# Value tiles of a Perceiver block's cross-attention: the tails of two batches in one tile

## What is computed

```
x = x + xattn(layernorm(x), ctx)          # 16 heads of 32; the change lies here
x = x + linear_attention(layernorm(x))
x = x + top2_of_8_experts(layernorm(x))

xattn:  q = xn @ Wq + bq;  kv = ctx @ Wkv + bkv      # k and v interleaved in the last axis
        p = softmax(q k^T / sqrt(32));  o = p v;  out = o @ Wout + bout
```

## Time and profile before

| | us |
|---|---|
| median of 3 runs | 2366.27 |
| lowest and highest | 2365.36, 2366.97 |
| the profiled execution | 2365.71 |
| its span | 2364.0 |
| TensorE matmuls busy (12921) | 2278.3 (96%) |
| weight loads | 1985.5 (84%) |
| VectorE busy | 1345.2 (57%) |
| GpSimd busy | 1109.5 (47%) |
| ScalarE busy | 1036.3 (44%) |

### The profile page before, as it was taken

How to read it: one execution, slowest core, us unless ns; L and a number is a source line. 1 busy time by engine, 2 the same in 40 slices (tenths; PEclk the granted TensorE clock), 3 DMA queues, 4 the chain that set the end, 5 groups by cost and what they waited for, 6 DMA issues and landing times. The chain is left out here.

```text
span 2364.0 us, 37285 instructions
## 1 busy us (share of the span) xinstructions
PE 2278.3 (96%) x12921; PEld 1985.5 (84%) x12921; DVE 1345.2 (57%) x2111; ACT 1036.3 (44%) x1737; POOL 1109.5 (47%) x456
## 2 busy tenths in 40 slices
PE   8999999999999999999999999999998897899996
PEld 7688889898888888898888888898876686888885
DVE  3155655565655656565656556565667546766652
ACT  3154444444444444444444444444445321545443
POOL 2155555454555555555554555554556202533334
PEclk9999999999999999999999999999999998999998
DMA  4212111121111121111111111121140102856643
GB/s 145 96 53 56 47 48 45 49 63 50 48 47 48 47 59 58 48 45 49 58 55 47 47 48 45 53 66 48 45 132 19 39 25 107 244 179 194 189 149 83
DMA packets 141464, 175.61 MB, mean 74 GB/s; under 512 B 81600, under 2 KB 105024, under 8 KB 141248
## 3 DMA queue, kind: packets, MB, share of 16 engines
q1 hardware_dynamic: 132352, 147.37, 20.7%
q10 hardware_dynamic: 4608, 16.78, 2.2%
q0 software_dynamic: 4288, 8.67, 1.8%
HBM read 135.12 MB, written 37.65 MB: 73 GB/s over the span
## 5 line engine op out<-in xcount | busy, mean ns | idle before, releaser
L504 POOL TENSOR_TENSOR k_parts<-k_t,k_parts 64x1602 fp32r<-64x1602 f32 x128 | 436.8, 3412 | 720.1 <-DVE k_parts L588 720.1
L960 PE MATMUL ps_kv<-ctx_hi,wk_hi 128*128 128x384 f32 (+1 forms) x1024 | 376.0, 367 | 9.3 <-DVE ctx_lo L785 9.3
L652 DVE TENSOR_TENSOR probs_t<-ps_pt,probs_t 128x512 fp32r<-128x512 f32 x376 | 207.7, 553 | 277.3 <-ACT probs_t L830 275.9
L960 PE MATMUL ps_kv<-ctx_hi,wk_lo 128*128 128x384 f32 (+1 forms) x1024 | 352.7, 344 | 0.0
L960 PE MATMUL ps_kv<-ctx_lo,wk_hi 128*128 128x384 f32 (+1 forms) x1024 | 352.7, 344 | 0.0
L960 PE MATMUL ps_kv<-wv_hi,ctx_hi 128*128 128x512 f32 (+1 forms) x832 | 342.8, 412 | 0.6 <-DVE wv_lo L755 0.6
L960 PE MATMUL ps_kv<-wv_lo,ctx_hi 128*128 128x512 f32 (+1 forms) x832 | 330.5, 397 | 0.0
L960 PE MATMUL ps_kv<-wv_hi,ctx_lo 128*128 128x512 f32 (+1 forms) x832 | 326.3, 392 | 0.0
L838 ACT ACTIVATE probs_both<-ps_s,neg_max 128x1601 f32<-128x1601 f32 x128 | 205.1, 1602 | 178.9 <-DVE neg_max L638 178.9
L818 ACT ACTIVATE k_t<-ps_kv,bk_sb 128x384 f32<-128x384 f32 (+1 forms) x256 | 152.5, 596 | 294.8 <-PE ps_kv L960 294.8
L493 POOL TENSOR_TENSOR ctx_lo<-ctx_raw,ctx_hi 128x1536 fp32r<-128x1536 f32 (+1 forms) x64 | 233.7, 3651 | 86.0 <-DVE ctx_hi L577 84.6
(11 more groups left out here) (315 smaller groups left out, 4079.3 us busy)
## 6 DMA issues: line engine op xcount, KB each, us to landing
ctx_raw<-ctx_dram SPq DMA_DIRECT2D x49, 768.0 KB, 4.7
w_raw<-w_dram SPq DMA_DIRECT2D x64, 512.0 KB, 4.5
rows_in<-zeros SPq DMA_DIRECT2D x150, 128.0 KB, 4.1
w_raw<-w_dram ACTq DMA_DIRECT2D x32, 512.0 KB, 4.5
ctx_raw<-ctx_dram SPq DMA_DIRECT2D x16, 900.0 KB, 4.9
q_blocks<-q_parts SPq DMA_DIRECT2D x256, 32.0 KB, 2.4
rows<-rows_in SPq DMA_DIRECT2D x8, 768.0 KB, 4.7
q_parts<-probs_t SPq DMA_DIRECT2D x16, 256.0 KB, 2.0
```

Of the source, the lines that this page charges most:

```text
L504: nc.gpsimd.tensor_tensor(k_parts[64 - 64 * s:128 - 64 * s, :], k_t[par][64 * s:64 * s + 64, g, :], k_parts[64 * s:64 * s + 64, :].bitcast ...
L652: nc.vector.tensor_tensor(probs_t[0:m, j:j + k, 1, :], ps_turned[kv][g][0:m, 0:k, :], probs_t[0:m, j:j + k, 0, :].bitcast(F32), ALU.subtra ...
L960: last = nc.tensor.matmul(o, still, moving, start=(k == 0 and i == 0), stop=(k == DT - 1 and i == 2))
```

## The change

Odd batches no longer make their thirteenth value unit. The last value tile of an even batch b has 128 context columns instead of 65: its own last 65 rows and 63 of the 65 last rows of batch b+1 (unit kind "T"). The result is copied whole into `v[0]`, and two DMA transfers on SP then bring the odd batch's rows to `v[1]`: 63 rows from `v[0]`'s partitions 65 to 127, and 2 rows from a small array in DRAM, `ends_v`. These last two rows of all eight odd batches (16 rows) are made by one small group of 12 matmuls at the beginning, ahead of unit 14 (`values_of_ends`).

The columns of a T unit come from an array `tails` of their own (2304 bytes in each of 128 partitions a batch), laid out on the host, with its own buffers `tail_raw`, `tail_hi`, `tail_lo`, loaded in pair 1 and split in pair 3 of odd batches (`TAILS_AT`), and once at the start. For odd batches unit 27 counts twice in `kv_done` and `kv_copied`, so that all later counts stay as they are.

```diff
+ENDS = 2 * (TAIL - P // 2) * (B // 2)
+TAIL_W = DT * (P + ENDS)
-    vs = [("V", min(j * P // CW, CHUNKS - 1), j) for j in range(JT)]
+    vs = [("V", j * P // CW, j) for j in range(JT - 1)] + [("T", CHUNKS - 1, JT - 1)]
...
+        TURN_FROM, QUERY_FROM, ENDS_FROM = 8, 16, 14
+        ends = o_t[0:ENDS].rearrange("p g c -> p (g c)")
+        ends_bank = ps_s[0:ENDS, 3 * BANK:4 * BANK]
...
+        TAILS_AT = 3
+        def has_unit(par, n):
+            return par == 0 or n < NU - 1
+        def units_ended(par, n):
+            return 2 if par == 1 and n == NU - 2 else 1
...
         @block.sync
+            def load_tails(b):
+                if positive(b):
+                    sp.wait_ge(kv_done, NU * (b - 1))
+                sp.dma_start(tail_raw[:], tails[b] if isinstance(b, int) else tails[bass.ds(b, 1)].rearrange("a p n -> (a p) n")
+                             ).then_inc(tail_loaded, 16)
+            def move_tails(b):
+                sp.wait_ge(kv_copied, NU * b)
+                sp.wait_ge(moved, 16)
+                if positive(b - 1):
+                    sp.wait_ge(v_lo_done, PAIRS * (b - 1))
+                half = TAIL - 2
+                sp.dma_start(v[1][0:half, JT - 1, :], v[0][TAIL:P, JT - 1, :]).then_inc(moved, 16)
+                sp.dma_start(v[1][half:TAIL, JT - 1, :], ends_v[bass.ds(b - 1, 2), :]).then_inc(moved, 16)
...
+                    if p == 2 and par == 0:
+                        move_tails(b + 1)
+                    if p == 1 and par == 1:
+                        load_tails(b + 1)
...
             sp.dma_start(wq_sb, wq.rearrange("(t p) n -> p t n", p=P)).then_inc(wq_loaded, 16)
+            load_tails(0)
             for c in range(2, CHUNKS):
                 load_ctx(0, c)
+            sp.wait_ge(w_hi_done, DT + 2)
+            sp.dma_start(ends_v, ends).then_inc(moved, 16)
...
         @block.gpsimd
+            def split_tails(b):
+                pool.wait_ge(tail_hi_done, b + 2)
+                nc.gpsimd.tensor_tensor(tail_lo[:], tail_raw[:], tail_hi[:].bitcast(F32), ALU.subtract
+                                        ).then_inc(tail_lo_done, 2)
+                pool.wait_ge(tail_lo_done, b + 2)
...
+                    if p == TAILS_AT and par == 1:
+                        pool.wait_ge(k_lo_done, n + 3)
+                        pool.wait_ge(ctx_lo_done, chunks)
+                        split_tails(b + 1)
...
-            for c in range(1, CHUNKS):
+            split_ctx(0, 1, 0)
+            pool.wait_ge(ctx_lo_done, 2)
+            split_tails(0)
+            for c in range(2, CHUNKS):
...
         @block.vector
+            def round_tails(b):
+                dve.wait_ge(tail_loaded, 8 * (b + 2))
+                nc.vector.tensor_copy(tail_hi[:], tail_raw[:]).then_inc(tail_hi_done, 2)
...
                     for b_of, c in splits_at(b, p, kv):
                         split_ctx(b_of, c)
+                    if p == TAILS_AT and par == 1:
+                        round_tails(b + 1)
...
             split_ctx(0, 1)
+            round_tails(0)
             norm_x()
...
         @block.scalar
+                elif kind == "T":
+                    if positive(b):
+                        act.wait_ge(moved, 16 + 16 * b)
+                    nc.scalar.copy(v[par][:, which, :], ps_kv[bank][:]).then_inc(kv_copied, 1)
...
                 if p == 0:
                     act.wait_ge(kv_copied, NU * (b + 1))
+                    if par == 1:
+                        act.wait_ge(moved, 16 + 16 * (b + 1))
...
+                    if k == ENDS_FROM:
+                        nc.scalar.copy(ends, ends_bank).then_inc(w_hi_done, 1)
...
         @block.tensor
+                if kind == "T":
+                    pe.wait_ge(tail_lo_done, b + 2)
...
+                    elif kind == "T":
+                        o, tile = bank[:], slice(k * P, (k + 1) * P)
+                        passes = [(tail_hi[:, tile], wv_hi[:, k, :]), (tail_hi[:, tile], wv_lo[:, k, :]),
+                                  (tail_lo[:, tile], wv_hi[:, k, :])]
...
-                last.then_inc(kv_done, 1)
+                last.then_inc(kv_done, units_ended(par, n))
+            def values_of_ends():
+                pe.wait_ge(tail_lo_done, 2)
+                for k in range(DT):
+                    hi, lo = (part[:, DT * P + k * ENDS:DT * P + (k + 1) * ENDS] for part in (tail_hi, tail_lo))
+                    for i, (still, moving) in enumerate([(hi, wv_hi), (hi, wv_lo), (lo, wv_hi)]):
+                        nc.tensor.matmul(ends_bank, still, moving[:, k, :], start=(k == 0 and i == 0),
+                                         stop=(k == DT - 1 and i == 2))
...
                         for u in AT[p][gap] if kv else ():
-                            unit(b + 1, 1 - par, u)
+                            if has_unit(1 - par, u):
+                                unit(b + 1, 1 - par, u)
...
+                    if k == 3:
+                        pe.wait_ge(w_hi_done, DT + 2)
```

More of the change, by code:

```diff
@@ L116 @@
 LAST = CHUNKS - 1
-START += [unit for g in range(DT) for unit in (("K", LAST, g), ("V", LAST, JT - DT + g))]
+START += [unit for g in range(DT) for unit in (("K", LAST, g), ("V" if g < DT - 1 else "T", LAST, JT - DT + g))]
 START_LAST_OF_CHUNK = [max(n for n, u in enumerate(START) if u[1] == c) for c in range(CHUNKS)]
@@ L131, in positive, with build @@
     return not isinstance(value, int) or value > 0
-def build(nc, x, ctx, wq, bq, wk, wv, bk, bv, wout, bout, lwq, lwk, lwv, lwo, router, w1, w2, out):
+def build(nc, x, ctx, tails, wq, bq, wk, wv, bk, bv, wout, bout, lwq, lwk, lwv, lwo, router, w1, w2, out):
     q_parts = nc.dram_tensor("q_parts", (2, D, NT), F32, kind="Internal").ap()
@@ L137, in build @@
     inv_t = nc.dram_tensor("inv_t", (B, PAIRS, 2, LQ), F32, kind="Internal").ap()
+    ends_v = nc.dram_tensor("ends_v", (ENDS, D), F32, kind="Internal").ap()
     rows_in = nc.dram_tensor("rows_in", ((B - 1) * ZERO_PIECES * ZERO_ROWS, D), F32, kind="Internal").ap()
@@ L142, in build @@
         shared = Shared(nc)
-        cross_attention(nc, ident, shared, x, ctx, wq, bq, wk, wv, bk, bv, wout, bout, lwq, lwk,
-                        q_parts, attn_t, inv_t, rows_in)
+        cross_attention(nc, ident, shared, x, ctx, tails, wq, bq, wk, wv, bk, bv, wout, bout, lwq, lwk,
+                        q_parts, attn_t, inv_t, ends_v, rows_in)
         m = Tail(nc, whole, shared)
@@ L209, in cross_attention @@
             ctx_raw.append(nc.alloc_sbuf_tensor_at(f"ctx_raw{i}", shape, F32, offset=at))
+        tail_hi = sb("tail_hi", [P, TAIL_W], F32R)
+        at = -(-nc.sbuf_base // 32) * 32
+        tail_lo = mem.enter_context(nc.sbuf_tensor("tail_lo", [P, TAIL_W], F32R, align_bytes=32))
+        tail_raw = nc.alloc_sbuf_tensor_at("tail_raw", [P, TAIL_W], F32, offset=at)
         k_t, v = [sb("k_t0", [P, DT, LC2])], [sb("v0", [P, JT, D])]
@@ L287, in cross_attention @@
         rows_zeroed = sem("rows_zeroed")
+        tail_loaded, tail_hi_done, tail_lo_done, moved = sem("tail_loaded"), sem("tail_hi"), sem("tail_lo"), sem("moved")
         wout_loaded, bout_loaded, lwq_loaded, lwk_loaded = (
@@ L316, in start_steps @@
                     yield "scores", 0
+                if u == ENDS_FROM:
+                    yield "ends", 0
                 yield "unit", u
@@ L661, in batch @@
                         dve.wait_ge(o_stored, 64 * b)
+                    elif p == 1:
+                        dve.wait_ge(moved, 16)
                     if positive(n):
@@ L819, in copy_unit @@
                                          bias=bk_sb[:, which:which + 1]).then_inc(kv_copied, 1)
+                elif kind == "T":
+                    if positive(b):
+                        act.wait_ge(moved, 16 + 16 * b)
+                    nc.scalar.copy(v[par][:, which, :], ps_kv[bank][:]).then_inc(kv_copied, 1)
                 else:
                     m = rows(which)
-                    nc.scalar.copy(v[par][0:m, which, :], ps_kv[bank][0:m, :]).then_inc(kv_copied, 1)
+                    nc.scalar.copy(v[par][0:m, which, :], ps_kv[bank][0:m, :]).then_inc(kv_copied, units_ended(par, n))
             def copy_group(n, g, kv):
@@ L915, in _ @@
                         nc.scalar.activation(std[:], std[:], ACT.Sqrt).then_inc(std_done, 1)
+                    if k == ENDS_FROM:
+                        nc.scalar.copy(ends, ends_bank).then_inc(w_hi_done, 1)
                 elif kind == "exponent":
                     exponent(0, 0)
-                elif kind == "scores":
+                elif kind in ("scores", "ends"):
                     pass
@@ L939, in unit @@
                 bank = ps_kv[(NU * par + n) % 2]
-                if n == 0 or order[n - 1][1] != c:
+                if kind == "T":
+                    pe.wait_ge(tail_lo_done, b + 2)
+                elif n == 0 or order[n - 1][1] != c:
                     pe.wait_ge(ctx_lo_done, CHUNKS * b + c + 1)
@@ L1085, in _ @@
                     unit(0, 0, k)
+                elif kind == "ends":
```

(9 more changed lines are left out.)

8 lines of the change are left out of this document (4 added, 4 removed).

## The result

The changed kernel takes 2376.79 us (median of 5 runs, 2375.16 to 2377.59), the kernel before 2365.36 us on the same chip (5 runs, 2362.43 to 2366.97): a ratio of 1.005, 95% interval 1.0039 to 1.0061, 11.4 us slower. The forecast was 2371.3 us, 5.0 slower: the right side and inside the range, with less than half of the loss. The profiled executions are 9.5 us apart (spans 2373.5 and 2364.0 us).

The account below looks back on a forecast made before the run. TensorE, busy 96% of the span, was taken to bound the kernel. Terms 2.8 + 2.1 + 9.9 + 1.7 - 11.5 = +5.0 us on 2366.27 gave 2371.3 us, range 2364 to 2377.

Parts of the forecast that it names:

- The jumps: Six loop jumps after even batches 2 to 12: removed units come back only 1.45 us each, 8.7 us saved.
- The holes: TensorE's stops before the transposes of L1005 at the six jumps, forecast to grow to 1.6 to 2.1 us.
- The rival of the cheaper jump: TensorE's jump costs less than its record: 2.8 to 7.9 us less, 2366.8 us at 2.8 with no clock fall; 15%.
- Batch 0 into 1: First removed unit, where no jump is taken: transposes come earlier by the unit's whole time, 2.77 us saved.
- The held cast in the loop: VectorE's tail cast at pair 3, seven odd batches, held by GpSimd's k_parts: 1.4 us late each, 9.9 us.
- 10.9 us: The seven held casts by the skill page alone, fully blocked: 7 x 1.55 us instead of 7 x 1.4.
- The start: Before the loop: small unit's 12 matmuls +2.8 us; VectorE's tail cast, held by GpSimd, makes unit 8 late, +2.1 us.
- The last unit: Removed unit of batch 14: worth nothing, since the last batch goes by VectorE and TensorE only waits 2.8 us longer.
- moves: SP's two SBUF copies at pair 2 and load at pair 1: nothing, at most 0.5 us in all.
- The clock: TensorE's clock may fall after the six holes at the jumps; one fall taken, 1.7 us; bounds none and six.
- three and four falls of the clock: Rival: clock falls at three or more holes, or in the start's wait too: +8.4 to +13.5 us; 17%.

Follow-up runs that it names:

- the kernel before written out: Kernel before with its loop over the batches written out, so no engine jumps between batches: 2359.1 us, ratio 0.9971.
- the removal alone: Kernel before with only the odd batches' thirteenth value unit and its ScalarE copy left out, context load released earlier: 2462.6 us, total not comparable; six jumps -0.9 us.
- the extra copy: Kernel before plus a 768 KB DRAM-to-DRAM copy issued by SP once in each odd batch, near VectorE's jump: 2365.2 us, ratio 1.0.
- the load moved: Changed kernel with SP holding the context load at odd batches' first pair until VectorE's first output step behind its jump: 2373.0 us, ratio 1.0042.
- four mends: Changed kernel with both tail casts on ScalarE, the context load behind VectorE's jump, and divisions behind the second remainder: 2357.2 us, 0.9962; batches written out, 2342.5 us, 0.989.
- the kernel with ScalarE's later jump: Changed kernel with ScalarE waiting for an even batch's last values before its jump: 2384.1 us, ratio 1.0073.

## Why the forecast was right or wrong

- *The jumps: wrong, the step that failed.* "VectorE's outputs start at 1100.47, behind its own jump, and end at 1101.5, before the second transposes at 1102.4. Saved 6 x 1.45 = 8.7 us": this took VectorE's 2.95 us for a property of the jump. It depends on what else is on the DMA queues. The removal raises the unit's semaphore one unit earlier, the context load that it guards goes out 0.6 us ahead of VectorE's jump, the jump lasts 4.6 to 5.5 us, and at five of six the gain is lost again in a wait for `o_t` (6.7 us in all); at the sixth the clock fell. Measured: -0.4 us for the -7.0 forecast (8.7 saved, less the one clock fall that I had put at 1.7). I had asked which engines come to the jump earlier, not which transfers.
- The holes themselves were right: 1.4 to 1.9 us each, 9.9 us in six (forecast 1.6 to 2.1 each). The rival of the cheaper jump is out: TensorE's ends at 1106.6, 1.1 us behind its last matmul, and lasts 3.3 to 3.9 us (3.5 to 4.1 before).
- *Batch 0 into 1: mis-sized*, 1.6 for 2.77 us. I compared the end of the divisions with where the transposes would come, and had VectorE run as before; GpSimd's v_parts, earlier by the removed unit too, holds the second division. With the divisions moved the whole 2.77 us came.
- *The held cast in the loop: right*, 10.7 for 9.9 us. The Trainium skill (SBUF — State Buffer, on the shared port pair) has the loser fully blocked; its 10.9 us was nearer than my 9.9, and the rows above (3.35 us for a cast that takes 0.45 unheld, ended 0.31 us behind GpSimd) agree with it but for the little done before the hold.
- *The start:* small unit 2.8, cast 2.1 forecast. The cast ended at 25.2 us (forecast 25.35), unit 8 came at 32.55 (forecast 33.1) and the stop ahead of it is 1.44 us; the shift was 3.8 us, with a scatter as large as what is missing.
- *The last unit, moves:* right at nothing. The last batch goes by VectorE after as before: from values to its fourth transposes 9.87 us (1759.62 to 1769.49), 9.92 before.
- *The clock:* one fall, as taken. The rest of the loop ran 1.9 us faster (1.2 to 2.0 in the others with the shared tile and the loop, 1.4 in the kernel before written out, not in the removal alone); why stays open. The difference of 9.5 us between the profiled spans is 1.1 us less than at the loop's end, and that too is unexplained.
- *Inside the range by luck.* The upper half of the range was laid out for three and four falls of the clock; there was one, and the loss came from the jumps, for which the forecast had no rival that cost time but the clock.

The Trainium skill (Runtime: NRT & Kernel Launch, Instruction fetch mechanics) says that each sequencer fetches its instructions by a DMA queue of its own and that a taken branch out of the fetched window stalls it. The stops that go when the loop is written out agree with the second. Of the first, the trace shows q8 behind TensorE's jumps alone, but q14 behind both ScalarE's and VectorE's, so here these two share a queue. That a fetch stands behind a data load on another queue is what the experiments and the packets above show.

## What to carry over

When a unit of work is removed, follow every semaphore that it raised: buffers come free earlier, and the load they release can land on a jump, a fetch or a transfer that was alone until then. A stall that a trace shows has the length it has beside today's neighbours; before it is used as a constant, look at what else is moving while it lasts. And an instruction that is held by another engine belongs where a hold is already being paid, or on an engine that isn't held.

## What was not expected

- Over all kernels with the loop (for ScalarE the one with the extra copy apart), VectorE's jump lasts 2.8 to 3.2 us when it begins before a 768 KB transfer is issued or at most 0.2 us behind it, and 4.5 to 5.6 us when it begins 0.5 to 0.7 us behind a context load; ScalarE's 2.5 to 3.5 us when it begins beside the load or before it, and 3.6 to 4.5 us when 1.3 to 1.4 us behind.
- Three engines fetching at once cost nothing extra: with the load moved, TensorE, ScalarE and VectorE are at their jumps together, and these last 3.4 to 3.8, 2.6 to 2.8 and 2.8 to 3.0 us (before, with ScalarE apart: 3.6 to 4.2, 2.6 to 3.0 and 2.8 to 3.1).
- The clock fell behind some of the holes at the jumps only: once in six in the changed kernel (idle up to 1.9 us), twice with four mends and three times in the removal alone (up to 2.3 us in both). The length of the hole doesn't decide: one of 1.8 us in the removal alone was followed by a fall, one of 2.1 us in the kernel with ScalarE's later jump was not.
